# A transformer kernel on one core: the query/key rotation moved wholly to VectorE and one tick later, and TensorE's value products moved to the end of a tick

## The chip, the cores and the metric

The kernel runs on 1 core of one Trainium2 chip. The metric is the device time of one execution in microseconds (us), median of three runs. The granted clock of TensorE, given with a run, is a share of 2.4 GHz.

## The reference, cut to what matters

Sixteen sequences of 256 tokens with 128 features pass two layers, each `x = x + s * silu(f)` over a layer norm of x. In the first, s is a causal attention with 16 heads of 64 and f a router with 8 experts beside a shared feed-forward part. In the second, s is a linear attention and f a transformer of two layers of its own, with a local attention of 8 heads. The change is in this local attention's queries and keys:

```python
qkv = h @ wqkv
q, k, v = jnp.split(qkv, 3, axis=-1)
q = l2norm(q) * qs
k = l2norm(k) * ksc
# rotary_xpos
q = q * cos * scale + rotate_half(q) * sin * scale
k = k * cos / scale + rotate_half(k) * sin / scale
o = local_attention(q, k, v)
```

`rotate_half` swaps the two halves (32 elements each) of each head and changes the sign of one.

## The kernel before, in words

The work is cut into 8 blocks of 512 tokens (4 tiles of 128). Both attentions (kind 0: the causal one; kind 1: the local one, with part 0 and part 1 for its two inner layers) are cut into 256 steps. A step is two heads of one sequence. A `Plan` written by rules lays the steps on some 340 ticks, some of them without a step (None), and puts the other work (`side`) on numbered ticks. Every engine runs through the same ticks in order, with a queue of its own, and they meet through semaphores. There is no scheduler beyond that: what stands in a tick of an engine is in the order of its loop.

A step takes three ticks on TensorE: `logits` in its tick, `transposes` of the probabilities one tick later, `values` (the products with v, lines 567 and 570) two ticks later, and after the second step of a pair `merge` (line 577, it lays out the reciprocal denominators). VectorE does `masked` (line 974) in the step's tick, half of the copies (line 984) one tick later, `scaled` (line 995) three ticks later. ScalarE does `exps` (lines 811 and 812), half of the copies (line 825), and the copy of `merge` (rT, line 789).

The side work that the change touches: `qkv b l t` projects tile t of block b for inner layer l. TensorE makes three 512-wide products (line 669) into the `mm` ring, which has two PSUM banks, so that the third waits until ScalarE has emptied the first. ScalarE writes the square (`sq`, line 888) and the value (`raw`, line 889) of queries and keys, and v. VectorE sums the squares (`ss`, line 1158) and multiplies raw by the cosine table into `qkr` (line 1163). GpSimd multiplies the swapped halves of raw by the sine table into `sq` (lines 1377 and 1378). One tick later VectorE adds the two in `rot` (line 1168). `raw` and `sq` have two buffers, so ScalarE's evacuation of tile t waits for `rot` of tile t-2:

```python
        if j >= 2:
            act.wait_ge(c.rot_ready, j - 1)
```

After the fourth tile `rr` (lines 1173 to 1175 and the Newton steps at 267 to 272) makes the reciprocal norms, `kn` (line 1259) scales the keys, and the transposes of the new queries (line 530) may begin. Each block has eight such tiles, four for each inner layer. In the first inner layer (`l` 0) they stand in ticks with steps of an attention, beside `lin` and `phi` of the linear attention (line 1129 is VectorE's part of `phi`). In the second (`l` 1) most of their ticks have no step.

Other side work named below: `yT` (line 505) transposes the normalized h, which GpSimd whitens (line 291); `glu` (lines 715 and 717) is the gated part, with ScalarE's Gelu at line 910; `v` (line 511) makes the first attention's values; `cum` (lines 678 and 680) belongs to the linear attention, `down1` to the inner feed-forward part.

Of the kernel before, what the change touches and what calls it, by code (L numbers as in the profile page):

```python
# [7 lines left out]
ALU = mybir.AluOpType  # L8
# [3 lines left out]
P = 128  # L12
# [93 lines left out]
class Plan:  # L106
# [31 lines left out]
    def qkv_stages(self, at, b, l):  # L138
        for t in range(TILES):
            self.put(at + t, "qkv", b, l, t)  # L140
        self.put(at + TILES, "rr", b, l)
        for t in range(TILES):
            self.put(at + t + 1, "rot", b, l, t)
        self.put(at + TILES + 1, "kn", b, l)
# [149 lines left out]
def buffers(nc, ctx, c):  # L294
# [3 lines left out]
    def sem(name):  # L298
        return ctx.enter_context(nc.semaphore(name))
# [116 lines left out]
        sem(n + "_ready") for n in ("xn1", "mn", "ex", "phi", "kv", "o1"))  # L416
    c.ss_ready, c.t2_ready, c.rot_ready, c.r_ready, c.kn_ready = (sem(n + "_ready") for n in ("ss", "t2", "rot", "r", "kn"))
    c.xag_ready, c.hn_ready, c.fin_th, c.out_ready = (sem(n) for n in ("xag_ready", "hn_ready", "fin_th", "out_ready"))
# [10 lines left out]
def count_units(c, plan):  # L429
# [14 lines left out]
    for tick in range(plan.length):  # L444
# [5 lines left out]
        if st := plan.step(tick - 1):  # L450
            for h in range(2):
                pt.add(("t", st.n, h), lane=h)
        if st := plan.step(tick - 2):
            if st.s == 0:
                o.add(("o", st.pair))
            else:
                mm.add(("m", st.pair))
        for seg in plan.side.get(tick, ()):
            for ring, n in USES.get(seg[0], {}).items():
                for j in range(n):  # L460
                    rings[ring].add((*seg, j))
            plan.combs[seg] = combs
            combs += seg[0] == "comb"
            if seg[0] in ("ln1", "ln2"):
                plan.whitened[seg] = tuple(whitened)
            elif seg[0] in ("ln1n", "ln2n"):
                plan.whitened[seg] = sum(whitened) + 1
                whitened[seg[0] == "ln2n"] += 1
    return mm, s, pt, o

# [13 lines left out]
def tensor(nc, pe, c, plan, mm, s, pt, o):  # L484
# [276 lines left out]
    for tick in range(plan.length):  # L761
# [4 lines left out]
        if plan.step(tick - 1):  # L766
            transposes(plan.step(tick - 1))
        if st := plan.step(tick - 2):
            values(st)
            if st.s == 1:  # L770
                merge(st.pair)
        if tick == 4:
# [3 lines left out]
        for seg in plan.side.get(tick, ()):  # L776
            if seg[0] in stage:
                stage[seg[0]](*seg[1:])


def scalar(nc, act, c, plan, mm, s, pt, o):
# [148 lines left out]
    for tick in range(plan.length):  # L930
# [4 lines left out]
        if plan.step(tick - 1):  # L935
            copies(plan.step(tick - 1))
        if (st := plan.step(tick - 2)) and st.s == 1:
            merge(st.pair)
        if tick == 4:
            act.wait_ge(c.p1_loaded, c.P1_LOADS)  # L940
            act.wait_ge(c.hT_zero, 1)
        for seg in plan.side.get(tick, ()):
            if seg[0] in stage:
                stage[seg[0]](*seg[1:])


def vector(nc, dve, c, plan, mm, s, pt, o):
# [205 lines left out]

    def qkv(b, l, t):
        g = LAYERS * b + l
        dve.wait_ge(c.mm_done, mm.done("qkv", b, l, t, 1))
        at = t * 2 * HEADS1
        TR(c.ss[:, at:at + 2 * HEADS1], c.sq[:, t % 2, :].rearrange("p (g d) -> p g d", d=HD), axis=AX.X, op=ALU.add)\  # L1158
            .then_inc(c.ss_ready, 1)
        if t == 0 and g:  # L1160
            dve.wait_ge(c.mm_full, mm.full("k", last_pair(plan, 1, (g - 1) // 2, (g - 1) % 2)))
        four_ = lambda a: a.rearrange("p (a h d) -> p a h d", a=2, h=HEADS1)
        link(TT(four_(c.qkr[:, t, :]), four_(c.raw[:, t % 2, :]),  # L1163
                c.rots[:, l, t % 2, 0, :, :].unsqueeze(2).to_broadcast([P, 2, HEADS1, HD]), ALU.mult))

    def rot(b, l, t):
        dve.wait_ge(c.t2_ready, (LAYERS * b + l) * TILES + t + 1)
        TT(c.qkr[:, t, :], c.qkr[:, t, :], c.sq[:, t % 2, :], ALU.add).then_inc(c.rot_ready, 1)  # L1168
# [28 lines left out]
    def fin(b):  # L1197
# [9 lines left out]
    stage = {"wo": wo, "ffn": ffn, "down0": down0, "comb": comb, "route": route, "tables": tables, "eg": eg, "ln1": ln1,  # L1207
             "ln1n": ln1n, "ln2": ln2, "ln2n": ln2n, "phi": phi, "sum": total, "o1": o1, "s1": s1, "qkv": qkv, "rot": rot,
             "rr": rr, "kn": kn, "glu": glu, "down1": down1, "fin": fin}
# [52 lines left out]
def gpsimd(nc, pool, c, plan, mm, s, pt, o, dram):  # L1262
# [106 lines left out]

    def qkv(b, l, t):  # L1370
        j = (LAYERS * b + l) * TILES + t
        pool.wait_ge(c.mm_done, mm.done("qkv", b, l, t, 1))
        pool.wait_ge(c.ss_ready, j + 1)
        src = c.raw[:, t % 2, :].rearrange("p (a h d) -> p a h d", a=2, h=HEADS1)
        dst = c.sq[:, t % 2, :].rearrange("p (a h d) -> p a h d", a=2, h=HEADS1)
        tab = c.rots[:, l, t % 2, 1, :, :].unsqueeze(2).to_broadcast([P, 2, HEADS1, HD])
        G.tensor_tensor(dst[:, :, :, 0:H2], src[:, :, :, H2:HD], tab[:, :, :, 0:H2], ALU.mult)  # L1377
        G.tensor_tensor(dst[:, :, :, H2:HD], src[:, :, :, 0:H2], tab[:, :, :, H2:HD], ALU.mult).then_inc(c.t2_ready, 1)

    def kn(b, l):  # L1380
# [6 lines left out]
    def shift(b, l):  # L1387
# [3 lines left out]

    stage = {"scatter": scatter, "wg": wg, "r": r, "xn": xn, "tables": tables, "lin": lin, "kv": kv, "qkv": qkv,
             "kn": kn, "shift": shift, "cum": cum, "ln1n": ln1n, "ln2n": ln2n}

# [200 lines left out]
```

## Time and profile before

| what | value |
|---|---|
| median of 3 runs | 2353.08 us (2352.51 to 2355.82) |
| the profiled execution | 2357.51 us |
| its span, first to last instruction | 2355.6 us |
| what lies around the span | 1.9 us |
| mean granted clock of TensorE | 0.904 |
| busy share of the span | TensorE 80%, VectorE 55%, ScalarE 53%, GpSimd 36% |

The busy shares are averages over ticks with different limits. What a tick is limited by is read from its own rows: which engine starts last and for whom it waited. A time in brackets behind a row is the idle time of the engine ahead of the instruction, with what ended it.

### The profile page before, as it was taken

What the parts mean: (1) busy time and instruction counts of PE and PEld (TensorE: products, weight loads), DVE (VectorE), ACT (ScalarE), POOL (GpSimd) and SP (SyncE); (2) the same over time, 40 slices, a digit from 0 to 9 for tenths busy, and PEclk for the clock granted to TensorE, in tenths of its full rate; (3) what the DMA queues carried; (4) which work ended last, traced back from release to release, by engine and by line L of the source; (5) the groups of instructions that cost most, each with busy time, mean ns of one, the idle gap of its engine ahead of it and who ended that gap; (6) DMA issues with size and microseconds to landing.
All of it is one profiled execution on the core that took longest, in us unless ns stands there. A gap on an engine that the chain in (4) does not pass through costs nothing.

```text
span 2355.6 us, 34690 instructions
## 1 busy us (share of the span) xinstructions
PE 1896.2 (80%) x10900; PEld 1178.0 (50%) x10900; DVE 1287.8 (55%) x4083; ACT 1239.2 (53%) x3559; POOL 838.0 (36%) x912
## 2 busy tenths in 40 slices
PE   5599987986798878986899679976898779857866
PEld 4378754553355345553456335543555436534534
DVE  4345446545655546555754564545654565556644
ACT  2455545653565556555555555554664456445434
POOL 2722234324432433224431343224332443244431
PEclk9799999997899988998999799997899789968878
DMA  7155400000000000000000000000000000000000
GB/s 222 45 182 155 143 19 5 1 1 5 1 1 15 4 2 1 15 1 1 5 10 5 1 1 1 19 1 1 1 10 5 1 1 1 6 4 1 5 0 5
DMA packets 49711, 53.26 MB, mean 23 GB/s; under 512 B 6386, under 2 KB 42236, under 8 KB 49532
## 3 DMA queue, kind: packets, MB, share of 16 engines
q0 software_dynamic: 7808, 27.79, 3.5%
q1 hardware_dynamic: 41724, 23.26, 3.4%
q8 instruction: 91, 1.49, 0.3%
q14 instruction: 88, 0.72, 0.1%
HBM read 41.60 MB, written 9.44 MB: 22 GB/s over the span
## 4 chain that ended last, share of the span: by engine, by line
PE 52%; DVE 17%; ACT 15%; issue 12%; POOL 4%; DMA 1%; DVEq 0%; SPq 0%; ACTq 0%; POOLq 0%
PE ps L551 5%; PE ps L595 5%; PE ps L567 4%; PE ps L543 4%; PE ps L520 4%; PE ps L540 3%; DVE big L1163 3%; ACT p L811 3%; ACT p L812 3%; PE ps L669 2%; DVE p L974 2%; ACT big L888 2%; PE ps L511 2%; PE ps L530 2%; PE ps L715 2%
## 5 line engine op out<-in xcount | busy, mean ns | idle before, releaser
L811 ACT ACTIVATE p<-p,nmax 128x128 f32<-128x128 f32 x512 | 201.7, 394 | 421.4 <-DVE nmax L974 420.8
L669 PE MATMUL ps<-wqkv,hT 128*128 128x512 f32 x384 | 224.8, 699 | 137.4 <-ACT big L889 87.7
L974 DVE CUSTOM_DVE_ANT_0 p<-ps,mask,nrq 128x128 f32<-128x128 f32 (+1 forms) x512 | 182.7, 412 | 215.6 <-PE ps L543 215.3
L1377 POOL TENSOR_TENSOR big<-big,rots 128x512 f32<-128x512 f32 x64 | 132.5, 2070 | 385.7 <-DVE ss L1158 375.6
L551 PE MATMUL ps<-ident,p 128*128 128x128 f32 x1536 | 248.3, 300 | 10.9 <-DVE ff L1021 4.9
L974 DVE CUSTOM_DVE_ANT_0 p<-ps,mask 128x128 f32<-128x128 f32 (+1 forms) x512 | 152.2, 353 | 186.2 <-PE ps L543 171.2
L1273 POOL COPY rdx<-rden 128x256 f32<-128x256 f32 x256 | 95.0, 400 | 446.3 <-DVE rden L990 446.2
L812 ACT ACTIVATE p<-p,nmax 128x256 f32<-128x256 f32 x512 | 252.4, 493 | 0.0
L551 PEld LDWEIGHTS ps<-ident,p 128*128 128x128 f32 x1536 | 179.6, 150 | 109.3 <-issue 93.3
L669 PEld LDWEIGHTS ps<-wqkv,hT 128*128 128x128 f32 x384 | 69.7, 210 | 249.8 <-ACT big L889 144.0
L530 PE MATMUL ps<-ident,big 128*128 128x128 f32 x512 | 93.9, 326 | 123.8 <-DVE big L1168 79.1
L540 PEld LDWEIGHTS ps<-k,q 64*128 64x128 f32 x1024 | 86.3, 203 | 185.2 <-issue 111.4
L567 PE MATMUL ps<-pt,v 128*64 128x256 f32 x1024 | 177.2, 426 | 0.0
L543 PE MATMUL ps<-k,q 64*128 64x256 f32 x1024 | 172.3, 413 | 0.0
L1343 POOL TENSOR_TENSOR big<-big,qkb 128x360 f32<-128x360 f32 (+1 forms) x96 | 82.5, 859 | 246.5 <-ACT big L839 246.3
L540 PE MATMUL ps<-k,q 64*128 64x128 f32 x1024 | 137.7, 347 | 39.7 <-DVE nmax L974 22.4
L1158 DVE TENSOR_REDUCE ss<-big 128x16 f32<-128x1024 f32 x64 | 78.1, 1220 | 165.2 <-ACT big L889 165.2
L530 PEld LDWEIGHTS ps<-ident,big 128*128 128x128 f32 x512 | 70.3, 167 | 157.4 <-issue 115.8
L789 ACT ACTIVATE q<-ps 128x512 f32<-128x512 f32 x128 | 76.0, 594 | 138.4 <-PE ps L530 81.4
L984 DVE COPY pt<-ps 128x384 f32<-128x384 f32 x256 | 141.2, 552 | 6.6 <-PE ps L551 6.6
L595 PE MATMUL ps<-wo,attT 128*128 128x128 f32 x1024 | 131.9, 292 | 9.1 <-DVE attT L995 7.5
L595 PEld LDWEIGHTS ps<-wo,attT 128*128 128x128 f32 x1024 | 129.6, 208 | 14.5 <-issue 10.5
(214 smaller groups left out, 4049.1 us busy)
## 6 DMA issues: line engine op xcount, KB each, us to landing
slots_in<-xn SPq DMA_DIRECT2D x1, 2560.0 KB, 13.7
v<-slots_in SPq DMA_DIRECT2D x20, 128.0 KB, 4.8
slots_out<-v SPq DMA_DIRECT2D x20, 128.0 KB, 1.8
big<-in_x SPq DMA_DIRECT2D x4, 512.0 KB, 6.4
x<-in_x SPq DMA_DIRECT2D x8, 256.0 KB, 3.7
out_x<-x SPq DMA_DIRECT2D x8, 256.0 KB, 2.3
wqkv<-in_wqkv SPq DMA_DIRECT2D x2, 768.0 KB
xn<-in_x SPq DMA_DIRECT2D x6, 256.0 KB, 3.3
```

The costliest lines, as they stand in the source:

```text
L530: last = nc.tensor.transpose(bank[:, t * P:(t + 1) * P], c.qkr[:, t, a:a + P], c.ident[:, :])
L540: MM(banks[h][:, 0:P], q[f:f + HD, 0:P], k[f:f + HD, 0:P], start=True, stop=True)
L543: MM(banks[h][:, P:SB], q[f:f + HD, P:SEQ], k[f:f + HD, :], start=True, stop=True).then_inc(c.s_full, 1)
L551: last = nc.tensor.transpose(bank[:, j * P:(j + 1) * P], c.p[:, u % 4, j * P:(j + 1) * P], c.ident[:, :])
L567: MM(bank[f:f + HD, q:q + SEQ], v[:, 2 * st.s, a:a + HD], pts[h][:, 0:SEQ], start=True, stop=False)
L595: last = MM(bank[:, t * P:(t + 1) * P], c.attT[kind][:, i, t * P:(t + 1) * P], w, start=i == 0, stop=i == LAST)
L669: MM(bank[:, :], c.hT[:, t * P:(t + 1) * P], c.wqkv[:, l, i * INNER1:(i + 1) * INNER1], start=True, stop=True).then_inc(c.mm_full, 1)
L811: A(p[:, 0:P], p[:, 0:P], ACT.Exp, bias=c.nmax[:, u % 4, 0:1], scale=-1.0, accum_out=den[:, 0:1])
L812: A(p[:, P:SB], p[:, P:SB], ACT.Exp, bias=c.nmax[:, u % 4, 1:2], scale=-1.0, accum_out=den[:, 1:2])\
L974: last = V.tensor_tensor_reduce(out=c.p[:, u % 4, a:b], in0=bank[:, a:b], in1=c.mask[st.kind][:, P * (1 - i):SEQ], scale=scale, scalar=3e3 ...
L984: V.tensor_copy(c.pt[:, u % 4, :], bank[:, 0:SB]).then_inc(c.pt_done, 1)
L1377: G.tensor_tensor(dst[:, :, :, 0:H2], src[:, :, :, H2:HD], tab[:, :, :, 0:H2], ALU.mult)
```

## The change

In the plan the part of `qkv` that VectorE did becomes a segment of its own, `mix`, one tick after the projection; `rot` follows it in the same tick. GpSimd's two products go to VectorE, which now does, for a tile: the sum of squares, raw times the cosine table (into `sq`, over the squares, so it waits for the sum), the two half-width products with the sine table (into `qkr`), and the sum. The last tile's `mix` stands ahead of `rr`. The semaphore between GpSimd and VectorE goes.

Apart from that, TensorE's `values` and `merge` of a tick, which stood between the transposes and the side work, now stand behind the side work. ScalarE's copy for `merge` moves in the same way, and the order of the PSUM ring follows.

```diff
     def qkv_stages(self, at, b, l):
         for t in range(TILES):
             self.put(at + t, "qkv", b, l, t)
-        self.put(at + TILES, "rr", b, l)
         for t in range(TILES):
+            self.put(at + t + 1, "mix", b, l, t)
+            if t == TILES - 1:
+                self.put(at + TILES, "rr", b, l)
             self.put(at + t + 1, "rot", b, l, t)
         self.put(at + TILES + 1, "kn", b, l)
...
             transposes(plan.step(tick - 1))
-        if st := plan.step(tick - 2):
-            values(st)
-            if st.s == 1:
-                merge(st.pair)
...
                 stage[seg[0]](*seg[1:])
+        if st := plan.step(tick - 2):
+            values(st)
+            if st.s == 1:
+                merge(st.pair)
...
-    def qkv(b, l, t):
-        g = LAYERS * b + l
+    def mix(b, l, t):
         dve.wait_ge(c.mm_done, mm.done("qkv", b, l, t, 1))
         at = t * 2 * HEADS1
         TR(c.ss[:, at:at + 2 * HEADS1], c.sq[:, t % 2, :].rearrange("p (g d) -> p g d", d=HD), axis=AX.X, op=ALU.add)\
             .then_inc(c.ss_ready, 1)
+        dve.wait_ge(c.ss_ready, (LAYERS * b + l) * TILES + t + 1)
+        four_ = lambda a: a.rearrange("p (a h d) -> p a h d", a=2, h=HEADS1)
+        TT(four_(c.sq[:, t % 2, :]), four_(c.raw[:, t % 2, :]),
+           c.rots[:, l, t % 2, 0, :, :].unsqueeze(2).to_broadcast([P, 2, HEADS1, HD]), ALU.mult)
+        g = LAYERS * b + l
         if t == 0 and g:
             dve.wait_ge(c.mm_full, mm.full("k", last_pair(plan, 1, (g - 1) // 2, (g - 1) % 2)))
-        four_ = lambda a: a.rearrange("p (a h d) -> p a h d", a=2, h=HEADS1)
-        link(TT(four_(c.qkr[:, t, :]), four_(c.raw[:, t % 2, :]),
-                c.rots[:, l, t % 2, 0, :, :].unsqueeze(2).to_broadcast([P, 2, HEADS1, HD]), ALU.mult))
+        src, dst = four_(c.raw[:, t % 2, :]), four_(c.qkr[:, t, :])
+        tab = c.rots[:, l, t % 2, 1, :, :].unsqueeze(2).to_broadcast([P, 2, HEADS1, HD])
+        TT(dst[:, :, :, 0:H2], src[:, :, :, H2:HD], tab[:, :, :, 0:H2], ALU.mult)
+        link(TT(dst[:, :, :, H2:HD], src[:, :, :, 0:H2], tab[:, :, :, H2:HD], ALU.mult))
 
     def rot(b, l, t):
-        dve.wait_ge(c.t2_ready, (LAYERS * b + l) * TILES + t + 1)
         TT(c.qkr[:, t, :], c.qkr[:, t, :], c.sq[:, t % 2, :], ALU.add).then_inc(c.rot_ready, 1)
...
-    def qkv(b, l, t):
-        j = (LAYERS * b + l) * TILES + t
-        pool.wait_ge(c.mm_done, mm.done("qkv", b, l, t, 1))
-        pool.wait_ge(c.ss_ready, j + 1)
-        src = c.raw[:, t % 2, :].rearrange("p (a h d) -> p a h d", a=2, h=HEADS1)
-        dst = c.sq[:, t % 2, :].rearrange("p (a h d) -> p a h d", a=2, h=HEADS1)
-        tab = c.rots[:, l, t % 2, 1, :, :].unsqueeze(2).to_broadcast([P, 2, HEADS1, HD])
-        G.tensor_tensor(dst[:, :, :, 0:H2], src[:, :, :, H2:HD], tab[:, :, :, 0:H2], ALU.mult)
-        G.tensor_tensor(dst[:, :, :, H2:HD], src[:, :, :, 0:H2], tab[:, :, :, H2:HD], ALU.mult).then_inc(c.t2_ready, 1)
```

VectorE, block 2, first inner layer, the tick in which tile 2 is projected, from its first copy to the next tick's `masked`. Before:

```order
L984 COPY pt<-ps4 128x384
L1129 SCALAR_TENSOR_TENSOR qkb<-qkb,mn 128x256
L1158 TENSOR_REDUCE ss<-big 128x16
L1163 TENSOR_TENSOR big<-big,rots 128x1024
L1168 TENSOR_TENSOR big<-big 128x1024
L974 ISA p,nmax<-ps3,mask1,nrq 128x128
```

The same piece of the changed kernel:

```order
L985 COPY pt<-ps4 128x384
L1130 SCALAR_TENSOR_TENSOR qkb<-qkb,mn 128x256
L1158 TENSOR_REDUCE ss<-big 128x16
L1162 TENSOR_TENSOR big<-big,rots 128x1024
L1169 TENSOR_TENSOR big<-big,rots 128x16x32
L1170 TENSOR_TENSOR big<-big,rots 128x16x32
L1173 TENSOR_TENSOR big<-big 128x1024
L975 ISA p,nmax<-ps3,mask1,nrq 128x128
```

Two products of half width have come in. Not to be seen in the rows: the sum of squares, the products and the sum now all belong to the tile projected one tick before, where the first two belonged to this tick's.

TensorE, block 2, the tick with `yT` of block 1's second inner layer (line 505, 506 after), from its `transposes` (551, 552) to the next tick's `logits` (540, 541). Before:

```order
L551 MATMUL ps5<-ident,p 128x128 x3
L567 MATMUL ps7<-pt,v1 64x256 x2
L570 MATMUL ps7<-pt,v1 64x128 x2
L577 MATMUL ps1<-ident,rdx 128x128 x4
L505 MATMUL ps0<-ident,h 128x128 x4
L678 MATMUL ps1<-big,tri 128x360
L680 MATMUL ps1<-big,tri 128x360
L520 MATMUL ps0<-xnT,wq 128x512
L540 MATMUL ps2<-k,q 128x128
```

After:

```order
L552 MATMUL ps5<-ident,p 128x128 x3
L506 MATMUL ps1<-ident,h 128x128 x4
L679 MATMUL ps0<-big,tri 128x360
L681 MATMUL ps0<-big,tri 128x360
L568 MATMUL ps7<-pt,v1 64x256 x2
L571 MATMUL ps7<-pt,v1 64x128 x2
L578 MATMUL ps1<-ident,rdx 128x128 x4
L521 MATMUL ps0<-xnT,wq 128x512
L541 MATMUL ps2<-k,q 128x128
```

`values` and `merge` stood ahead of `yT`, the piece for which TensorE waits on GpSimd, and stand behind it and `cum` now.

## Rows read from the trace of the kernel before

**Rows 1.** The page: span.

```profile
span 2355.6 us, 34690 instructions
```

**Rows 2.** Groups by line and shape: count, busy us, mean ns, idle before.

```profile
L1377 POOL TENSOR_TENSOR big<-big,rots 128x512 f32<-128x512 f32 x64 | 132.5, 2070 | 385.7 <-DVE ss L1158 375.6 <-ACT v L789 9.9
...
L1168 DVE TENSOR_TENSOR big<-big 128x1024 f32<-128x1024 f32 x64 | 121.0, 1891 | 1.6
...
L1163 DVE TENSOR_TENSOR big<-big,rots 128x1024 f32<-128x1024 f32 x64 | 81.4, 1272 | 0.0
...
L1259 DVE TENSOR_TENSOR big<-big,rr 128x512 f32<-128x512 f32 x32 | 25.0, 821 | 0.1
```

**Rows 3.** Waits: total us, times, longest us.

```profile
ACT p L811 <- DVE nmax L974: 420.8, 233, 9.9
...
PE ps L505 <- POOL h L291: 58.1, 16, 7.8
```

**Rows 4.** Timeline, first inner layer, block 2: start us, us, engine, line.

```profile
867.75 0.40 ACT L811 ACTIVATE p<-p,nmax 128x128 f32<-128x128 f32 x1 [2.73 <-DVE nmax L974]
...
880.71 0.40 ACT L811 ACTIVATE p<-p,nmax 128x128 f32<-128x128 f32 x1 [4.87 <-DVE nmax L974]
...
882.84 0.40 ACT L894 ACTIVATE mn<-mn 128x256 f32<-128x256 f32 x1
...
883.28 0.43 DVE L1129 SCALAR_TENSOR_TENSOR qkb<-qkb,mn 128x256 f32<-128x256 f32 x1 [0.86 <-ACT mn L894]
...
885.21 1.22 DVE L1158 TENSOR_REDUCE ss<-big 128x16 f32<-128x1024 f32 x1 [1.51 <-ACT big L889]
...
886.35 1.22 DVE L1163 TENSOR_TENSOR big<-big,rots 128x1024 f32<-128x1024 f32 x1
...
887.60 2.18 DVE L1168 TENSOR_TENSOR big<-big 128x1024 f32<-128x1024 f32 x1
...
889.70 0.34 DVE L974 CUSTOM_DVE_ANT_0 p<-ps,mask,nrq 128x128 f32<-128x128 f32 x1
...
890.49 0.40 ACT L811 ACTIVATE p<-p,nmax 128x128 f32<-128x128 f32 x1 [3.52 <-DVE nmax L974]
...
900.87 0.40 ACT L811 ACTIVATE p<-p,nmax 128x128 f32<-128x128 f32 x1 [2.09 <-DVE nmax L974]
...
907.73 0.40 ACT L811 ACTIVATE p<-p,nmax 128x128 f32<-128x128 f32 x1 [4.14 <-DVE nmax L974]
```

**Rows 5.** Line 1168: durations, ns min/median/max.

```profile
L1168 DVE TENSOR_TENSOR big<-big x64: 1216/2168/2183, 371.0 to 2284.4; 128x1024 f32<-128x1024 f32 x64
```

**Rows 6.** Timeline, second inner layer, block 2: start us, us, engine, line.

```profile
1049.47 0.55 DVE L984 COPY pt<-ps 128x384 f32<-128x384 f32 x1
...
1055.62 2.17 DVE L1168 TENSOR_TENSOR big<-big 128x1024 f32<-128x1024 f32 x1
...
1062.30 2.17 DVE L1168 TENSOR_TENSOR big<-big 128x1024 f32<-128x1024 f32 x1
...
1071.68 0.64 DVE L1173 TENSOR_SCALAR ss<-ss 128x64 f32<-128x64 f32 x1
...
1075.23 1.22 DVE L1168 TENSOR_TENSOR big<-big 128x1024 f32<-128x1024 f32 x1
```

**Rows 7.** Timeline, a tick with `yT`: start us, us, engine, line.

```profile
945.00 0.65 PE L567 MATMUL ps<-pt,v 128*64 128x256 f32 x4
...
945.81 0.66 PE L577 MATMUL ps<-ident,rdx 128*128 128x128 f32 x4
...
948.85 0.91 PE L505 MATMUL ps<-ident,h 128*128 128x128 f32 x4 [2.38 <-POOL h L291]
```

**Rows 8.** Timeline, the next tick, with `glu`.

```profile
958.50 1.02 PE L717 MATMUL ps<-xT,g 128*114 128x512 f32 x2
...
959.48 1.11 PE L715 MATMUL ps<-xT,g 128*113 128x512 f32 x2
```

**Rows 9.** Timeline, a tick with `v`.

```profile
980.79 3.77 PE L511 MATMUL ps<-wv,xnT 128*128 128x512 f32 x8 [2.69 <-ACT rT L789]
```

More of the change, by code:

```diff
@@ L416, in buffers @@
         sem(n + "_ready") for n in ("xn1", "mn", "ex", "phi", "kv", "o1"))
-    c.ss_ready, c.t2_ready, c.rot_ready, c.r_ready, c.kn_ready = (sem(n + "_ready") for n in ("ss", "t2", "rot", "r", "kn"))
+    c.ss_ready, c.rot_ready, c.r_ready, c.kn_ready = (sem(n + "_ready") for n in ("ss", "rot", "r", "kn"))
     c.xag_ready, c.hn_ready, c.fin_th, c.out_ready = (sem(n) for n in ("xag_ready", "hn_ready", "fin_th", "out_ready"))
@@ L452, in count_units @@
                 pt.add(("t", st.n, h), lane=h)
-        if st := plan.step(tick - 2):
[L454 to L457, printed above, removed]
+        if (st := plan.step(tick - 2)) and st.s == 0:
+            o.add(("o", st.pair))
         for seg in plan.side.get(tick, ()):
@@ L468, in count_units @@
                 whitened[seg[0] == "ln2n"] += 1
+        if (st := plan.step(tick - 2)) and st.s:
+            mm.add(("m", st.pair))
     return mm, s, pt, o
@@ L767, in tensor @@
             transposes(plan.step(tick - 1))
-        if st := plan.step(tick - 2):
-            values(st)
-            if st.s == 1:
-                merge(st.pair)
         if tick == 4:
@@ L936, in scalar @@
             copies(plan.step(tick - 1))
-        if (st := plan.step(tick - 2)) and st.s == 1:
-            merge(st.pair)
         if tick == 4:
@@ L944, in scalar @@
                 stage[seg[0]](*seg[1:])
+        if (st := plan.step(tick - 2)) and st.s == 1:
+            merge(st.pair)
 def vector(nc, dve, c, plan, mm, s, pt, o):
@@ L1207, in vector @@
     stage = {"wo": wo, "ffn": ffn, "down0": down0, "comb": comb, "route": route, "tables": tables, "eg": eg, "ln1": ln1,
-             "ln1n": ln1n, "ln2": ln2, "ln2n": ln2n, "phi": phi, "sum": total, "o1": o1, "s1": s1, "qkv": qkv, "rot": rot,
+             "ln1n": ln1n, "ln2": ln2, "ln2n": ln2n, "phi": phi, "sum": total, "o1": o1, "s1": s1, "mix": mix, "rot": rot,
              "rr": rr, "kn": kn, "glu": glu, "down1": down1, "fin": fin}
@@ L1390, in shift @@
         G.tensor_tensor(c.xa[:, :, :], c.xa[:, :, :], wide(c.gb2[:, l, :], TILES), ALU.add).then_inc(c.xag_ready, 1)
-    stage = {"scatter": scatter, "wg": wg, "r": r, "xn": xn, "tables": tables, "lin": lin, "kv": kv, "qkv": qkv,
-             "kn": kn, "shift": shift, "cum": cum, "ln1n": ln1n, "ln2n": ln2n}
+    stage = {"scatter": scatter, "wg": wg, "r": r, "xn": xn, "tables": tables, "lin": lin, "kv": kv, "kn": kn, "shift": shift, "cum": cum, "ln1n": ln1n, "ln2n": ln2n}
     pool.memset(c.zero[:, 0, :], 0.0).then_inc(c.zero_ready, 1)
```

## The prediction

> **What bounds the kernel now.** I read the page first: the span is 2355.6 us [rows 1], TensorE is busy in 80% of it, the other engines in about half or less. So TensorE bounds many ticks, but a fifth of the time it waits, and the change can only pay there. The list of waits says who waits: ScalarE's exponentials wait 420.8 us in total for VectorE's `masked`, and TensorE waits 58.1 us in 16 places for GpSimd's whitened h [rows 3]. Most of the first is harmless (ScalarE idles in ticks that TensorE bounds), so I went to the timeline of the ticks with a projection.
>
> The reader is to see a ring there [rows 4]. From one tick's exponentials (880.71) to the next (890.49) are 9.78 us, and no engine is busy that long. ScalarE does its exponentials, the Exp of `phi` (882.84) and the four evacuations of the projection; VectorE stands idle for the last of them (885.21, 1.51 us "<-ACT big"), then does sum of squares, product and `rot`, and only behind them, at 889.70, the next step's `masked`, for which ScalarE waits 3.52 us. VectorE works on this tick's tile, so the next step's attention waits for this tick's projection. The second inner layer has a ring without attention [rows 6]: `rot` to `rot` is 62.30 - 55.62 = 6.68 us, made of evacuation, sum, product and a `rot` of 2.17 us, after which ScalarE may evacuate again.
>
> **The rotation, first inner layer.** GpSimd loses 64 pairs of products, some 2.07 us each product [rows 2]. They are off the path except in one way: the two-input sum at line 1168 takes 1216 ns at best but 2168 ns in the median [rows 5], and in the timeline it is long (2.18) just where GpSimd's products run and 1.22 in the last tile, where none is left [rows 4, 6]. So `rot` should fall to 1.22. The Trainium skill says this too (SBUF — State Buffer, Who interferes with whom: a VectorE instruction with two SBUF inputs and a GpSimd instruction that reads SBUF exclude one another for a whole instruction), and the trace agrees with its 2168 against 1216 ns. That rule also speaks against the change, since VectorE now has four such instructions for a tile where it had two, and GpSimd's work for `lin` may hold each up.
>
> New on VectorE are two products of 128x512. The trace has no such shape with swapped halves. From below: half of line 1163's 1.22 us, 0.61. From above: line 1259, 128x512, 0.82 in the mean, partly beside GpSimd [rows 2]; and as the far end 1.22, if short runs of 32 elements cost as much as a full row. I take 0.65, since 1163 reads a broadcast table in the same way. A tile then costs VectorE 1.25 (sum, and the wait for it, since `sq` is overwritten) + 1.14 + 2 x 0.65 + 1.14 = 4.8 us, where it cost 1.14 + 1.24 + 2.1 = 4.5 (885.21 to 889.70).
>
> The gain is that none of it waits for this tick's evacuation. VectorE starts when `phi` is done: exponentials to the end of the Exp 2.57 (880.71 to 883.28), `phi` 0.4, tile 4.8, `masked` to the next exponentials 0.79 (889.70 to 890.49): 8.6 us instead of 9.78. For the five intervals:
> - the tick of tile 0 loses its sum and product from VectorE's path (2.4 us), but TensorE's next logits then come after the value products: I take a gain of 1.1 (0 to 2.4).
> - the tick of tile 1, before 12.96 (867.75 to 880.71), goes to 8.6 + 1.0, my allowance for GpSimd's `lin` beside the products (no row shows that meeting; from 0 to 2): gain 3.4.
> - tile 2: gain 1.2.
> - tile 3, before 10.38 (890.49 to 900.87): 9.3, because TensorE is near there with values, merge and a projection ahead of the logits: gain 1.1.
> - the tick after, before 6.86 (900.87 to 907.73), now carries sum and products (3.7) ahead of `rr`: loss 3.7.
>
> Sum: 3.1 us a block (bounds 1 and 5), 8 blocks: 25 us.
>
> **The rotation, second inner layer.** From the copy at 1049.47 to the end of `rr` and the last `rot` (1075.23 + 1.22) are 27.0 us, full of waits. After the change VectorE need not wait: the tile behind is always evacuated, and the evacuation of the next but one starts at each `rot`. Its own work is then the length: `masked` free some 0.35 earlier; two copies and a reciprocal 1.1; three tiles 14.5; `scaled` 0.6 (512 wide, as the half product); the last tile's mix 3.7; `rr` 3.55 (1071.68 to 1075.23); `rot` 1.2: 24.6 us, minus 0.35. Gain 2.7 us a block (bounds 1.5 and 3.5), 8 blocks: 22 us.
>
> **The value products last.** Nothing is added, so in a tick that TensorE fills it costs nothing, and the order only turns round. It costs where TensorE waits in the side work: before, the value products lay ahead of that wait and inside it; now they lie behind it. The row with `yT` shows it: the products begin at 945.00, merge at 945.81, and TensorE still waits 2.38 us for h [rows 7]. The end of the wait is set by VectorE's Newton steps and GpSimd's four whitenings, which the new order doesn't start earlier. So the full 0.81 + 0.66 = 1.4 to 1.5 us is exposed, in 13 of the 16 places (the others have no step two ticks before): 19 us. In `glu` TensorE's fifth product follows the fourth by 0.98 us (958.50 to 959.48), with hardly a wait [rows 8]; it can't start before the Gelu has emptied a bank, which hangs on the exponentials. Reaching it 0.8 earlier gains nothing and the values come after: 7 x 0.8 = 6 us. `v` already waits 2.69 us for ScalarE [rows 9]; some 7 such ticks at 0.7: 5 us. Sum 30 us. Bounds: nothing, if the pieces started earlier end their waits earlier; and 45, if more ticks are of that kind and the products run slower. After the wait the four transposes at 948.85 take 0.91 us, where the four at 945.81 take 0.66 [rows 7].
>
> The Trainium skill (TensorE: Matmul & The Clock Gate, What's actually happening) says that the array's clock is halved unless activity releases it. By that rule the longer waits for h would also slow what follows each; the 0.91 against 0.66 agrees, and it would add something like 0.3 to 0.8 us a place.
>
> **The sum.** 25 + 22 - 30 = 17 us of gain; I take 14, for the slower products behind the longer waits. The profiled execution took 2357.5 (span 2355.6 and 1.9 around it), 4.4 above the median of 2353.1, so its successor would be 2343.5 and the median 2339. I predict 2340 us.
>
> **Rivals.**
> - *TensorE takes over as the bound in the projection ticks.* The third product of a projection waits until ScalarE has emptied the first's bank, and values, merge and the next logits now stand behind it. In my estimate logits come 0.8 us before VectorE is ready; at the lower clock they would not. For it: the tick of tile 1 already runs slowly. Against it: VectorE's 8.6 us is long. Some 40 tiles with steps near them x 1.1 (0.8, and 0.66 in every second) are 45 us; it decides as soon as 15 of them are exposed, which eats the 17. All of them: 2353 - 17 + 45 = 2381; half: 2359. Slower.
> - *VectorE's new products are dear.* At 0.82 each, 64 x 2 x 0.17 = 22 us more: 2358, slower or the same. At 1.22 each, 73 us: 2409. A lock by GpSimd of 0.35 us a tile has the effect of the first. Less likely, as VectorE's plain products scale with size.
> - *Values last costs nothing.* The side work starts up to 1.5 us earlier in each tick, and if the chain behind it (shift, moments, whitening) follows, the waits end earlier too: 2353 - 47 = 2306. Against it: `masked` and the Newton steps stand in VectorE's queue behind the step's logits, not behind the side work.
> - *It does not do what it says*, because each ring only closes elsewhere: gain and loss cancel, 2350 to 2357.
>
> **Chances.** The forecast, 5 to 26 us of gain, 0.50 (0.47 of it clearly faster); the gain without the cost, beyond 26 us, 0.17; cancelled 0.10; the two slower ones together 0.23. Two runs of this kernel can be told apart from about 0.2%, 4.7 us. Faster by more than that: 0.64, within: 0.13, slower: 0.23. The likeliest case alone spans 2327 to 2348; the range for 8 in 10 takes in part of both sides: 2314 to 2364.
>
> **What would show it.** Line 1168's successor should have a median near 1.22 us, and the new half-width products 0.6 to 0.7. In the first inner layer the five intervals of the exponentials should read about 7.4, 9.6, 8.6, 9.3, 10.6; if the middle ones stay near 10 and TensorE's logits are what `masked` waits for, the first rival holds. From the copy to the last `rot` in the second inner layer should be about 24. TensorE's wait for h should grow from 58 to about 77 us in the list of waits, with the value products behind it; if it does not grow, the third rival holds. GpSimd's busy time should fall by some 250 us without any use. I am wrong if VectorE is idle between the products, or if the intervals elsewhere (`cum`, `wo`, the expert ticks), which I hold for unchanged, have moved.

## The result, and the profile after

The changed kernel takes 2319.91 us in the median (2315.65 to 2321.69), the kernel before took 2352.80 in the runs beside it. The ratio is 0.9856, with a 95% interval of 0.9839 to 0.9874: faster by 33 us, where 13 were forecast (2340 from 2353).

The page of the changed kernel, its span and the busy times of the engines:

```profile
span 2319.9 us, 34592 instructions
PE 1853.4 (80%) x10900; PEld 1158.3 (50%) x10900; DVE 1315.5 (57%) x4211; ACT 1238.3 (53%) x3559; POOL 593.3 (26%) x784
```

The groups of the rotation on VectorE (columns as in [rows 2]):

```profile
L1162 DVE TENSOR_TENSOR big<-big,rots 128x1024 f32<-128x1024 f32 x64 | 78.4, 1225 | 2.2
L1173 DVE TENSOR_TENSOR big<-big 128x1024 f32<-128x1024 f32 x64 | 78.3, 1223 | 1.7
L1158 DVE TENSOR_REDUCE ss<-big 128x16 f32<-128x1024 f32 x64 | 77.2, 1207 | 3.0 <-ACT big L890 3.0
L1169 DVE TENSOR_TENSOR big<-big,rots 128x512 f32<-128x512 f32 x64 | 45.4, 709 | 0.0
L1170 DVE TENSOR_TENSOR big<-big,rots 128x512 f32<-128x512 f32 x64 | 43.7, 683 | 0.0
```

The last sum (1173, before 1168) lasts 1.22 us, always, where it had a median of 2.17 [rows 5]; the new products last 0.71 and 0.68. The reducer waits for ScalarE's evacuation for 3.0 us in the whole kernel: VectorE's work on a tile no longer hangs on this tick's evacuation. GpSimd's busy time fell from 838.0 to 593.3 us: 245 where 250 were forecast.

The list of waits, the two rows that answer to [rows 3]:

```profile
ACT p L812 <- DVE nmax L975: 368.9, 232, 10.0
...
PE ps L506 <- POOL h L293: 78.3, 16, 7.8
```

TensorE's wait for h grew by 20.2 us, from 58.1. The timeline of the first inner layer, block 2, in the same stretch as [rows 4] (each first row of the exponentials, line 812, begins a tick):

```profile
850.54 0.40 ACT L812 ACTIVATE p<-p,nmax 128x128 f32<-128x128 f32 x1 [1.11 <-DVE nmax L975]
...
858.15 0.40 ACT L812 ACTIVATE p<-p,nmax 128x128 f32<-128x128 f32 x1 [1.85 <-DVE nmax L975]
...
866.97 0.40 ACT L812 ACTIVATE p<-p,nmax 128x128 f32<-128x128 f32 x1 [1.62 <-DVE nmax L975]
...
869.54 0.42 DVE L1130 SCALAR_TENSOR_TENSOR qkb<-qkb,mn 128x256 f32<-128x256 f32 x1 [0.86 <-ACT mn L895]
869.88 1.21 DVE L1158 TENSOR_REDUCE ss<-big 128x16 f32<-128x1024 f32 x1
...
873.59 1.22 DVE L1173 TENSOR_TENSOR big<-big 128x1024 f32<-128x1024 f32 x1
874.73 0.34 DVE L975 CUSTOM_DVE_ANT_0 p<-ps,mask,nrq 128x128 f32<-128x128 f32 x1
...
875.52 0.40 ACT L812 ACTIVATE p<-p,nmax 128x128 f32<-128x128 f32 x1 [3.24 <-DVE nmax L975]
...
884.94 0.35 DVE L975 CUSTOM_DVE_ANT_0 p<-ps,mask,nrq 128x128 f32<-128x128 f32 x1 [1.57 <-PE ps L544]
...
885.79 0.40 ACT L812 ACTIVATE p<-p,nmax 128x128 f32<-128x128 f32 x1 [1.11 <-DVE nmax L975]
...
896.17 0.40 ACT L812 ACTIVATE p<-p,nmax 128x128 f32<-128x128 f32 x1 [7.66 <-DVE nmax L975]
```

The differences of the starts are 7.61, 8.82, 8.55, 10.27 and 10.38 us; forecast were 7.4, 9.6, 8.6, 9.3 and 10.6, before they were 8.48, 12.96, 9.78, 10.38 and 6.86. The first of these began ahead of the rows of [rows 4]:

```profile
859.27 0.40 ACT L811 ACTIVATE p<-p,nmax 128x128 f32<-128x128 f32 x1 [1.11 <-DVE nmax L974]
```

In the tick of tile 2 VectorE runs without a gap from `phi` (869.54) to `masked` (874.73). Of the ticks in which VectorE has a tile's products, only the fourth lets `masked` wait for TensorE's logits (884.94, 1.57 us).

The second inner layer of the same block, to be held against [rows 6]:

```profile
1044.21 0.55 DVE L985 COPY pt<-ps 128x384 f32<-128x384 f32 x1
...
1053.78 1.23 DVE L1173 TENSOR_TENSOR big<-big 128x1024 f32<-128x1024 f32 x1
...
1058.63 1.23 DVE L1173 TENSOR_TENSOR big<-big 128x1024 f32<-128x1024 f32 x1
...
1067.19 1.22 DVE L1173 TENSOR_TENSOR big<-big 128x1024 f32<-128x1024 f32 x1
```

From the copy to the end of the last sum are 24.2 us, where 27.0 were needed; sum to sum is 4.85 us, where it was 6.68.

The tick with `yT` that answers to [rows 7]:

```profile
935.71 1.09 PE L506 MATMUL ps<-ident,h 128*128 128x128 f32 x4 [3.99 <-POOL h L293]
...
939.13 1.12 PE L568 MATMUL ps<-pt,v 128*64 128x256 f32 x4
...
940.61 0.66 PE L578 MATMUL ps<-ident,rdx 128*128 128x128 f32 x4
```

TensorE waits 3.99 us instead of 2.38, and the value products behind the wait take 1.12 us instead of 0.65.

So most of what I had said of single steps holds, and yet the gain is over twice the forecast.

### The profile page after: what moved, and what is told of

The parts are those of the page before. It is cut to its first block, busy times and chain, and to the rows that moved or that the text cites. A ratio compares the mean times of both kernels' runs of the same rounds, so it can differ in the third digit from the quotient of the medians.

```text
span 2319.9 us, 34592 instructions
## 1 busy us (share of the span) xinstructions
PE 1853.4 (80%) x10900; PEld 1158.3 (50%) x10900; DVE 1315.5 (57%) x4211; ACT 1238.3 (53%) x3559; POOL 593.3 (26%) x784
## 4 chain that ended last, share of the span: by engine, by line
PE 55%; DVE 18%; ACT 12%; issue 9%; POOL 4%; DMA 1%; DVEq 0%; SPq 0%; ACTq 0%; POOLq 0%
PE ps L596 5%; PE ps L568 5%; PE ps L552 4%; PE ps L544 4%; PE ps L521 4%; PE ps L541 4%; ACT p L812 3%; ACT p L813 3%; PE ps L670 3%; PE ps L531 3%; PE ps L512 2%; PE ps L578 2%; DVE ss L1158 2%; PE ps L725 2%; PE ps L679 2%
## 5 line engine op out<-in xcount | busy, mean ns | idle before, releaser
L670 PE MATMUL ps<-wqkv,hT 128*128 128x512 f32 x384 | 201.5, 634 | 103.8 <-ACT big L890 76.6
L552 PE MATMUL ps<-ident,p 128*128 128x128 f32 x1536 | 238.6, 292 | 5.8 <-ACT pt L826 2.0
L552 PEld LDWEIGHTS ps<-ident,p 128*128 128x128 f32 x1536 | 173.6, 146 | 100.0 <-issue 90.3
L670 PEld LDWEIGHTS ps<-wqkv,hT 128*128 128x128 f32 x384 | 63.5, 191 | 204.6 <-ACT big L890 129.4
L790 ACT ACTIVATE rT<-ps 128x512 f32<-128x512 f32 x128 | 75.9, 593 | 136.6 <-PE ps L578 136.4
L826 ACT ACTIVATE pt<-ps 128x384 f32<-128x384 f32 x256 | 120.1, 469 | 4.5 <-PE ps L552 4.2
```

The source lines that it names most:

```text
L552: last = nc.tensor.transpose(bank[:, j * P:(j + 1) * P], c.p[:, u % 4, j * P:(j + 1) * P], c.ident[:, :])
L670: MM(bank[:, :], c.hT[:, t * P:(t + 1) * P], c.wqkv[:, l, i * INNER1:(i + 1) * INNER1], start=True, stop=True).then_inc(c.mm_full, 1)
L790: A(dst, mm_bank(*name)[:, :], ACT.Copy).then_inc(c.mm_done, 1)
```

## The experiments

Times are medians; the kernel before, run beside each group, took 2351.86 (e1 to e4), 2353.10 (e5 to e8), 2356.87 (e9, e10) and 2353.11 us (e11). For sums by kind of tick I took, in each trace, the intervals between the first exponentials of consecutive steps (line 811 before), paired them tick by tick between two traces, and added the differences. One trace is one execution, and the kernel before, unchanged, took from 2341.99 to 2361.42 us in the 52 executions beside the experiments; so medians are compared first, within a group where that is possible, and sums of ticks only say where a difference sits.

**e1: the rotation alone.**

```diff
         if plan.step(tick - 1):
             transposes(plan.step(tick - 1))
+        if st := plan.step(tick - 2):
+            values(st)
+            if st.s == 1:
+                merge(st.pair)
...
-        if st := plan.step(tick - 2):
-            values(st)
-            if st.s == 1:
-                merge(st.pair)
```

> The changed kernel with the value products and the merge back in their old place, ahead of the side work; the rotation stays as changed. Theory A (my prices for the rotation were right, the cost of the value products was overpriced): before minus 47, some 2306 us, faster than the changed kernel's 2320 by 14. Theory B (the value products cost the 30 us that I priced, and the rotation gives more than priced): before minus 63, some 2290. Theory C (the value products last bring a gain of their own, and the rotation gives less than priced): 2325 to 2340, slower than the changed kernel. Theory D (the two parts need each other: with the value products ahead of the projection the next logits come too late for a VectorE that is now ready early): also slower than the changed kernel, but then the value products alone bring nothing either.

Measured: 2297.61 us, ratio 0.9763 (0.9749 to 0.9776), 54 below the kernel before and 22 below the changed kernel. The numbers lie between those of A and B: the rotation gives more than priced, and the value products' new place costs less. C and D are out.

**e2: the value products last, alone.** The kernel before, with the opposite edit.

> The kernel before with the value products and the merge last in each tick, nothing else changed. Theory A: before plus 14, some 2367 us. Theory B: before plus 30, 2383. Theory C: faster than before by 5 to 25, 2328 to 2348. Theory D: within 5 of before, though the changed kernel would lose without it.

Measured: 2355.39 us, ratio 1.0016 (1.0006 to 1.0025), 3.5 slower. The same move costs 22 us with the new rotation and 3.5 with the old. A to C had one cost for both; D had this figure, but e1 had refuted it. The ticks tell where the difference sits. In both pairs of traces (e2 against before, the changed kernel against e1) the ticks with `yT` of the second inner layer are longer by 9 us in sum (8.8 and 9.0) and those with `glu` by 5 to 6 (4.9 and 6.1). But the four projection ticks of the first inner layer, all blocks together, are 13.3 us shorter in e2, and 4.2 longer in the changed kernel against e1. In block 2 of the kernel before, the tick of tile 1, whose exponentials begin at 867.75 [rows 4]:

```profile
870.61 4.47 PE L669 MATMUL ps<-wqkv,hT 128*128 128x512 f32 x6 [2.53 <-ACT rT L789]
...
872.75 0.60 ACT L888 ACTIVATE big<-ps 128x512 f32<-128x512 f32 x1 [1.54 <-PE ps L669]
```

The same in e2:

```profile
862.32 1.02 PE L668 MATMUL ps<-wqkv,hT 128*128 128x512 f32 x2
...
862.74 0.40 ACT L810 ACTIVATE p<-p,nmax 128x128 f32<-128x128 f32 x1 [2.73 <-DVE nmax L973]
...
865.60 0.59 ACT L887 ACTIVATE big<-ps 128x512 f32<-128x512 f32 x1
```

Before, the projection needs the bank that ScalarE frees by copying `merge`'s result, and ScalarE does that only after its exponentials. With `merge` last, the first product is there before the exponentials begin, and the first evacuation starts 2.86 us after them instead of 5.00. As long as VectorE waits for this evacuation, the tick can be shorter by that.

**e3: the products on VectorE, but no delay.**

```diff
             self.put(at + t, "qkv", b, l, t)
+            self.put(at + t, "mix", b, l, t)
+        self.put(at + TILES, "rr", b, l)
         for t in range(TILES):
-            self.put(at + t + 1, "mix", b, l, t)
-            if t == TILES - 1:
-                self.put(at + TILES, "rr", b, l)
             self.put(at + t + 1, "rot", b, l, t)
```

> The changed kernel with all three rotation products on VectorE, but in the tick of their projection, behind this tick's evacuation; only the sum at the end stays a tick later, as before. If the delay of a tick is what pays, the ring of the projection tick stays closed, and VectorE has 1.3 us more in it for a tile (two products of 0.65) against 1.0 less for rot (2.18 to 1.22): 64 tiles x 0.3 = 20 us slower than before, changed by what the value products last do, so 2350 to 2375. If instead the engine was what paid (GpSimd's products held VectorE's), it comes near the changed kernel, 2320 to 2330.

Measured: 2383.18 us, ratio 1.0129 (1.0112 to 1.0145), 8 above the range given. Against e2, from which it differs in the engine of the two products (and in the buffer that takes the cosine product), it is 28 slower. The move to VectorE costs; against the changed kernel, which has the delay besides, it is 63 slower. The tick's delay brings all of the gain.

**e4: the value products first where they were forecast to cost.** The plan answers for each tick, and the ring, TensorE and ScalarE follow it:

```diff
+    def early(self, tick):
+        names = {seg[0] for seg in self.side.get(tick, ())}
+        return bool(names & {"yT", "glu", "v"})
```

> The changed kernel, but in ticks with yT, glu or v among the side work the value products and the merge come first, as before; in all others last. The trace of the changed kernel has these ticks longer by some 1.2 us (yT of the second inner layer, 8 of them), 1.0 (glu, 7), 0.6 (yT of the first inner layer) and 0.6 (v), some 26 us in all. If these are real costs of the order, the kernel comes to some 2295. If the time only moves into the ticks behind them, it stays at 2315 to 2325.

Measured: 2301.12 us, ratio 0.9785 (0.9771 to 0.9799), 19 below the changed kernel. These three kinds of tick carry most of the cost of the order; TensorE's wait for h is 60.0 us again.

**e5: last only where the ticks are shorter.**

```diff
+        segs = self.side.get(tick, ())
+        if any(seg[0] in ("yT", "glu", "v") or (seg[0] == "qkv" and seg[3] == 0) for seg in segs):
+            return True
+        return not any(seg[:2] == ("wo", 0) or seg[0] in ("down0", "shift") or (seg[0] == "phi" and seg[2] == 1) for seg in segs)
```

> The changed kernel with the value products and the merge last only in the ticks in which the traces of the changed kernel and of the rotation alone, laid side by side, show the last place to be the shorter one: ticks with wo of the first layer, down0 or shift, and those of the second projection tile; first in all others (yT, glu, v, the first projection tile, and what is left). If the value products' place acts tick by tick, as those differences say (wo of the first layer 0.9 each, down0 0.8 to 1.4, shift 0.2, second projection tile 0.5, the stretch with the last ffn and down0 of block 0 1.4), the kernel comes to 10 to 14 below the rotation alone (2297.6), some 2285. If a shorter tick is paid back by the next, it stays at 2295 to 2300.

Measured: 2284.51 us, ratio 0.9716 (0.9700 to 0.9733), 13 below e1 (2277.02 to 2287.29 against 2293.21 to 2297.97, so clear of the spread). Where the last place pays is seen in the two traces of a tick with `wo` of the first layer. In e1 (value products first):

```profile
1407.67 3.73 PE L597 MATMUL ps<-wo,attT 128*128 128x128 f32 x32
1412.28 0.49 PE L542 MATMUL ps<-k,q 64*128 64x128 f32 x4 [0.87 <-DVE s_sb L1006]
```

In the changed kernel (last):

```profile
1419.51 3.73 PE L596 MATMUL ps<-wo,attT 128*128 128x128 f32 x32
1423.17 0.65 PE L568 MATMUL ps<-pt,v 128*64 128x256 f32 x4
...
1424.56 0.49 PE L541 MATMUL ps<-k,q 64*128 64x128 f32 x4
```

The next logits need the bank of `wo`, which VectorE must empty first. TensorE waited 0.87 us for that; now the value products fill this wait, and the tick takes 7.29 instead of 8.20 us. In e5's trace the ticks with `wo` of the first layer and `down0` are shorter than in e1 by 7.7 us in sum. But those with `yT` of the second inner layer are shorter too, by 6.0, though in both runs the value products stand first there: three of the seven run at a granted clock of 1.00 instead of 0.80. Not all of the 13 is covered waits.

**e6: one more product for three of four tiles.**

```diff
+        if t < TILES - 1:
+            TT(four_(c.qkr[:, t + 1, :])[:, :, :, 0:H2], src[:, :, :, H2:HD], tab[:, :, :, 0:H2], ALU.mult)
```

> The changed kernel with one more half-width product on VectorE for three of four tiles (its result is overwritten later, the output is unchanged): 48 more of 0.71 us. If VectorE sets the length of the projection ticks, as I forecast, all of it shows: 48 x 0.71 = 34 us above the changed kernel, 2354. If TensorE took over as the bound in the first inner layer's projection ticks (my first rival), only the 24 of the second inner layer count at most: 2337 or less.

Measured: 2353.35 us, 33.4 above the changed kernel (0.70 for each of the 48). 34 were expected, at most 17 if TensorE had bound the first inner layer. In the traces 13.6 us lie in the first inner layer's projection ticks, so VectorE sets their length and my first rival is out. That the sum fits so well is in part luck: 11.1 us lie in the second inner layer, where 24 products of 0.68 us would be 16, and some of the rest in ticks without a new product, at a lower clock (0.902 against 0.912 in the mean).

**e7: the half products back on GpSimd, a tick ahead of VectorE.** They are written straight into `qkr`, so they need not wait for the reducer as they did before.

```diff
+    def qkv(b, l, t):
+        pool.wait_ge(c.mm_done, mm.done("qkv", b, l, t, 1))
...
+        dst = c.qkr[:, t, :].rearrange("p (a h d) -> p a h d", a=2, h=HEADS1)
+        G.tensor_tensor(dst[:, :, :, 0:H2], src[:, :, :, H2:HD], tab[:, :, :, 0:H2], ALU.mult)
+        G.tensor_tensor(dst[:, :, :, H2:HD], src[:, :, :, 0:H2], tab[:, :, :, H2:HD], ALU.mult).then_inc(c.t2_ready, 1)
...
     def rot(b, l, t):
+        dve.wait_ge(c.t2_ready, (LAYERS * b + l) * TILES + t + 1)
```

> The changed kernel with the rotation's two half products back on GpSimd, in the tick of their projection, straight into the result buffer; VectorE does the sum, the cosine product and the last sum a tick later. VectorE saves 1.39 us for a tile (0.71 + 0.68). If the delay alone is what pays and GpSimd's help is still worth having, the second inner layer gains up to 8 x 4 x 1.39 and the first some 0.5 to 1.4 a tile, 40 to 60 us in all: 2260 to 2280. If GpSimd's products (2.07 us each, 128 of them) hold VectorE's two-input operations again (2.17 us instead of 1.22, one or two in a tile), the 1.39 is given back, 64 x 0.95 x 1 to 2 against 64 x 1.39: 2290 to 2350. The row to read is the duration of VectorE's cosine product and last sum.

Measured: 2308.61 us, ratio 0.9813 (0.9797 to 0.9828), 11 below the changed kernel: between the two. The groups of the products and of the last sum in e7:

```profile
L1378 POOL TENSOR_TENSOR big<-big,rots 128x512 f32<-128x512 f32 x64 | 107.5, 1680 | 0.0
L1377 POOL TENSOR_TENSOR big<-big,rots 128x512 f32<-128x512 f32 x64 | 100.8, 1574 | 292.2 <-ACT big L890 292.0
L1167 DVE TENSOR_TENSOR big<-big 128x1024 f32<-128x1024 f32 x64 | 99.5, 1554 | 8.8 <-POOL big L1378 7.4
L1162 DVE TENSOR_TENSOR big<-big,rots 128x1024 f32<-128x1024 f32 x64 | 85.6, 1337 | 2.2
```

The last sum costs 0.33 us more than in the changed kernel and the cosine product 0.11, together 0.44 for a tile against the 1.39 saved. Giving up GpSimd's products was no gain. They had been dear where they lay, behind the reducer and beside the last sum, which lasted 1.89 us in the mean [rows 2]; here it lasts 1.55, and 1.22 alone. How much each of the two counted these runs don't separate.

**e8: the value products last only in the ticks with `phi`, old rotation.** The kernel before, with `early` true where there is no `phi`.

> The kernel before, with the value products and the merge last only in the ticks with phi, where the first inner layer's projection runs (4 ticks a block); the rotation is as before. In the run with the value products alone those ticks are shorter by 13.3 us in sum, above all the tick of the second tile (12.7 to 10.6): the projection's products come earlier on TensorE, and the ring from the evacuation over VectorE to the next logits with them. If so, the kernel is faster than before by 13, 2339; in the changed kernel that ring is open, and the same move costs there (about 4). If the 13 us only come with the other moves, 2350 to 2354.

Measured: 2338.14 us, ratio 0.9942 (0.9922 to 0.9962), 15 faster than before, with a wide spread (2332.11 to 2348.22). In the trace the projection ticks are 13.3 us shorter, as in e2. This is the part of the order's effect that the delayed rotation takes away.

**e9 to e11: the versions that these runs point to.** e9 has the places of e5 and the products of e7. In e10 GpSimd does only the first half product and VectorE the second. e11 is e7 with the value products first everywhere: of the change only the delay is left.

> The chosen places for the value products (2284.5 us) together with the half products back on GpSimd a tick ahead (which took 11.3 off the changed kernel). If the two add, 2273. They may add less: in the first inner layer's projection ticks the value products' place had taken part of what VectorE's shorter work would give; if TensorE bounds those ticks by then, 2277 to 2282.

> The same, but GpSimd does only the first of the two half products, VectorE the second. VectorE's tile is 0.7 us longer than in the run above, GpSimd's product is done 1.6 us earlier and meets VectorE's two-input operations less. If VectorE's own length counts, 64 tiles cost up to 0.7 each in the ticks that it bounds, 5 to 10 above the run above; if the meeting with GpSimd's products counts, it comes out level with it or below.

> The rotation a tick later with its half products back on GpSimd, a tick ahead, and the value products first in every tick, as in the kernel before: only the delay is left of the change. GpSimd's products were worth 11 us with the value products last everywhere, 31 with them at the chosen places. If the value products' place at the end of the ticks is what hides VectorE's shorter work, they are worth some 25 to 31 here too: 2297.6 minus 28, 2270. If 11 is their own worth and the rest belongs to the chosen places: 2286.

Measured: e9 2253.67 us, ratio 0.9562 (0.9547 to 0.9577); e10 2281.49, 0.9673 (0.9658 to 0.9688); e11 2269.95, 0.9645 (0.9623 to 0.9666). Both expectations for e9 missed: GpSimd's products are worth 31 us with the chosen places, not 11 or less. For e10 I had 5 to 10 above e9, and it is 28 above. Here is its row of the half product on VectorE:

```profile
L1183 DVE TENSOR_TENSOR big<-big,rots 128x512 f32<-128x512 f32 x64 | 61.5, 961 | 0.0
```

0.96 us instead of 0.68: this product meets GpSimd's. With the other three groups VectorE's tile is 4.83 us long, where it is 4.12 in e9; these 0.7 were expected. What I had too low is the number of ticks in which they count: the first inner layer's alone are 19 us longer in the trace. e11 came as expected, 28 below e1. So the delay with GpSimd's help is worth 83 us of 2353; the value products last everywhere then cost 39 (e7 against e11), at the chosen places they bring 16 (e9 against e11). Where two groups are compared some us are uncertain: by the ratios the 31 are 36, and the 16 are 20. From 2319.91 to 2253.67 is what the change left lying.

## Why the prediction was right in its parts and wrong in its sum

| | forecast | measured |
|---|---|---|
| rotation, first inner layer | -25 | -28 (ticks, e1 against before) |
| rotation, second inner layer | -22 | -24 (ticks, e1 against before) |
| the rest of the rotation's effect | 0 | -2 by the medians (e1: -54 in all); -8 in the two traces |
| value products last | +30 | +22 (changed kernel against e1) |
| allowance taken off the sum | +3 | none beside the row above |
| sum | -14 (2340 from 2353) | -33 |

**The rotation.** Right in mechanism and nearly in size. A tile costs VectorE 4.85 us (in the timeline above the sum of squares begins at 869.88, and `masked` at 874.73), where I had 4.8; the half products and the last sum came as priced. My allowance of 1.0 us for GpSimd's `lin` in the tick of tile 1 was too much: that tick took 8.82 instead of 9.6. The one row that shows the meeting:

```profile
863.45 0.88 DVE L1169 TENSOR_TENSOR big<-big,rots 128x512 f32<-128x512 f32 x1
```

0.88 against 0.68 in the next tick: `lin` costs 0.2 there. In the fourth tick it was the other way (10.27 instead of 9.3), because there TensorE is late; in blocks where its granted clock was 1.00 the same tick took 8.67. And in e1 the ticks with `xT` (4.5 us in sum) and with `lin` but no projection (3.0), which hold no work that was changed, are shorter too, where I had written of the intervals elsewhere "which I hold for unchanged".

**The value products last: the term that failed.** Where I looked, the sums were as priced. The wait for h was forecast at 77 us and is 78.3. The ticks that I named are longer by 27 us against e1 (yT 18, with what stands behind it in the ticks without a step; glu 6, v 3), where I had 19 + 6 + 5 = 30. The step that failed is the sentence "Nothing is added, so in a tick that TensorE fills it costs nothing". I took the move for neutral or bad everywhere; it is a gain wherever the next tick's logits or projection wait for a bank that another engine must empty. The ticks with `wo` of the first layer alone are shorter by 0.9 to 1.1 each and those with `down0` by 0.8 to 1.4, some 7 us in sum; with small gains and losses in the others 5 of the 27 come back, and e5 shows that such gains can be had alone. The bound "nothing, if the pieces started earlier end their waits earlier" had the wrong reason: nothing ended earlier, another wait was covered. Of the 20 us between forecast and result, 8 are this term (30 priced, 22 measured); the rotation makes 5, the ticks that I held for unchanged 2 or more, the allowance 3, all on the same side.

That the cost of `yT` was as priced is in part luck. I had priced the exposed work alone, 1.45 us a place at an unchanged clock. The tick with `yT` of block 1, in e1 and in the changed kernel (columns: us, busy times of PE, PEld, DVE, ACT, POOL with their instruction counts, granted clock, DMA share, GB/s):

```profile
926.89:933.74 6.85, 4.71 (x26) 2.79 (x28) 2.89 (x11) 4.45 (x13) 3.37 (x5) 1.00 0.01 2
```

```profile
933.89:943.87 9.98, 8.16 (x37) 4.80 (x38) 2.89 (x11) 4.68 (x14) 3.38 (x5) 0.66 0.00 0
```

It is longer by 3.1 us, and its clock fell from 1.00 to 0.66. Take this tick in blocks 0, 1, 2, 4 and 5 in all thirteen traces. With the value products first it lasts 6.85 us at 1.00 (14 of 40 ticks), 7.9 to 8.5 at 0.78 to 0.80 and 9.3 to 9.4 at 0.63 to 0.64 (three ticks). With them last, behind TensorE's wait for h, it lasts 9.0 to 9.3 at 0.81 or 0.82 and 9.6 to 10.5 at 0.66 or 0.67, and never runs at 1.00 (0 of 25). At nearly the same clock, near 0.8, the order costs 0.5 to 1.4 us; the rest of the cost is the clock, which the sum had only in its allowance.

**One cost for a move that depends on the other.** I worked the two halves out one by one and added them. With the old rotation the same order costs 3.5 us, since it shortens the projection ticks by 13; with the new rotation that ring is open, and the same ticks are longer by 4. Forecast and result would have been compared wrongly had I tried only e2: 3.5 instead of 22.

**The allowance.** I took 3 us off for slower products behind longer waits. They are slower: 1.12 instead of 0.65 us. But this lies in the 22 us already. TensorE's busy time in the whole fell, with the same products in it, from 1896.2 us before to 1862.0 in e1 and 1853.4 in the changed kernel, so no further loss shows in the sum; how much of the fall is the clock was not separated.

**The rivals.** That TensorE takes over is refuted by e6. That VectorE's new products are dear is refuted by their rows, 0.71 and 0.68. "Values last costs nothing" is refuted by e1 as a whole, though its time (2306) is 14 us off and my forecast's 20. That all cancels is refuted by the result.

## What the runs showed of the hardware

The granted clock moves ticks that nothing else touches. The tick with `xT` of block 5, in the kernel before and in e1, in which the order of its work is the same; windows with the columns as above:

```profile
1609.45:1617.20 7.75, 6.30 (x29) 4.54 (x28) 1.86 (x10) 5.09 (x15) 1.16 (x2) 0.50 0.01 2
```

```profile
1576.96:1583.21 6.25, 3.56 (x29) 2.60 (x30) 1.84 (x10) 4.98 (x15) 1.20 (x2) 1.00 0.01 3
```

VectorE is busy for the same time, ScalarE nearly so; TensorE takes 6.30 us at a granted clock of 0.50 (1.2 GHz) and 3.56 at 1.00 (2.4 GHz), and the tick lasts 7.75 or 6.25 us. This is so in every trace: the `xT` ticks of blocks 1 to 6 last 7.74 to 7.76 us wherever the clock is 0.50 (13 times) and 6.25 to 6.31 wherever it is 1.00 (21 times). The same kernel moves with it too: the kernel before took 2341.99 us in an execution with a mean clock of 0.914 and 2361.42 in one with 0.903. Between the kernels the clock of all executions was 0.897 to 0.904 in e3, 0.902 to 0.914 before, 0.912 to 0.914 in the changed kernel, 0.916 to 0.920 in e1, 0.917 to 0.923 in e5 and 0.923 to 0.926 in e9: by and large the shorter versions ran at the higher clock (e7, with 0.910 to 0.911, is an exception). Which of the two brings the other is not shown. The Trainium skill says (TensorE: Matmul & The Clock Gate, What's actually happening) that the slow clock is the default and that activity releases it; the rows agree in the two levels. Apart from the ticks with `yT`, which change of the order tips which tick was not settled. e6 and e7 have their `qkv` and `xT` ticks now at one level, now at the other, and this is a candidate for why GpSimd's products were worth 11 us in one order and 28 to 31 in the others; it was argued, not shown.

The meeting of VectorE and GpSimd costs both. In e9, GpSimd's minimum of `lin`, first beside nothing, then beside VectorE's two-input product:

```profile
835.88 0.84 POOL L1347 TENSOR_SCALAR mn<-qkb 128x256 f32<-128x256 f32 x1
...
842.67 1.84 POOL L1347 TENSOR_SCALAR mn<-qkb 128x256 f32<-128x256 f32 x1
```

0.84 and 1.84 us for the same work. I had reckoned with the loss on VectorE alone. The rule of the Trainium skill (SBUF — State Buffer, Who interferes with whom) is one of mutual exclusion, which agrees. It doesn't say that GpSimd's work should go: done a tick ahead, its products took 1.57 and 1.68 us in e7 instead of 2.07 [rows 2] for the first and 1.95 for the second, with 1.25 at best, so that about half of the meeting was avoided.

## What to carry to other kernels

Price a moved piece of work at both ends: not only what now waits behind it, but which wait at the old and at the new place it covered or covers, down to the bank that the next tick's first product needs. When two edits touch the same ring, work out the second with the first already made; the sum of two separate prices is wrong by what both would have gained. Where a move lets TensorE stand still for longer, look at the granted clock of that tick in both orders: here a part of the cost was the clock. And when a helper engine's work is in the way, try to move it in time before taking it away: here the delay was worth 83 us with the helper and 54 without.
